# Summing y by fp32 transposes in the layout of the output projection, a buffer of its own for VectorE's product with C, and one-pair buffers for dt

## The chip, the cores and the metric

One core of one Trainium2 chip runs the whole program. The metric is the device time of one execution in microseconds (us). TensorE, VectorE, ScalarE, GpSimd and SyncE (which issues all the DMAs) run side by side and meet in semaphores. In the profile they stand as PE (matmuls) and PEld (its weight loads), DVE, ACT, POOL and SP.

## The reference, cut to what matters

All is fp32. The input is 16 sequences of 512 positions and 256 features.

```python
xr = x @ in_proj_w.T;  xf, res = split(xr, 512)
u0 = silu(conv(xf) + b);  u1 = silu(conv_b(u0) + b_b)          # two directions, d = 0 and 1
for d:   delta, B, C = split(u_d @ x_proj_w[d].T, [16, 32])
         dt = softplus(delta @ dt_proj_w[d].T + dt_proj_b[d])  # 512 channels
         dA_cum = exp(reversed cumulative sum of dt * A)       # 16 states a channel
         xs = cumsum(dt * u_d * B * dA_cum) / (dA_cum + 1e-12)
         y_d = sum over the 16 states of xs * C + u_d * D[d]
y = (y_0 + y_1) * silu(res)
x = layernorm(x + y @ out_proj_w.T)
# then a soft mixture of experts (1024 slots of 16 experts, softmax over rows and over columns)
x = layernorm(x + moe(x))
```

## The kernel before, in words

There are three stages: sequence_stage (16 sequences, a hardware loop of one turn each), expert_stage and merge_stage. The change is in the first only.

**The scan.** A sequence is worked through in 128 tiles, two tiles to a step, so 64 steps. A tile is one state of one chunk of 128 channels, 128 channels on the partitions by 512 positions. The 64 steps are four parts of 16 states: channels 0 to 255 in direction 0, then in direction 1 (tiles 0 to 63), then channels 256 to 511 in both (tiles 64 to 127). One step i goes through all engines:

- GpSimd: g = dtu * B (`inputs`, L637), into a ring of three, two steps ahead.
- ScalarE: e = exp(dt * A) into PSUM (`decay`, L802) and a guard factor f by a tanh (`guard`, L812), a step ahead.
- VectorE: the scan over positions, in place in PSUM (`scan`, L1008), then z = (f + 1) * e into z_ring, a ring of three (`guarded`, L1025).
- GpSimd: v = z * C into v_ring, a ring of three (`times_c`, L646). On every eighth step (i % 8 == 4, `ON_DVE`) VectorE does this product itself (L1034), and writes it over the step's place in z_ring.
- TensorE: adds v to y in two PSUM banks by a matmul with the identity as weights (`add_state`, L1175), six tiles later (`Y_LAG`).

Before `guarded(i)` writes its place in z_ring, it waits in `z_slot_free` (L1010) for the step that had the place last. Was that a GpSimd step, it waits for GpSimd's product; was it a VectorE step, as it is for i % 8 == 7, it waits until TensorE has added the product (`v_used`). GpSimd's product in turn waits until TensorE has added the product that stood in its place of v_ring.

**The gate.** At tiles 70 and 6 (of the next turn) VectorE multiplies a pair of y banks with `res_gate` into `yg` (`y_gate`, L991), channels on the partitions.

**The side work.** Everything else of the sequence is a list of 70 slots, written out by hand in `timetable()`: projections, convolutions, dt, the output projection, and the mixture's logits, softmaxes and slot sums. The slots take two PSUM banks in turn. `slot_tiles` gives each slot a tile, from the weights in HOLD. At that tile TensorE fills the slot's bank (`fill`, L1077, after it has waited for the bank's last reader); two to five tiles later ScalarE and VectorE read it (`side_step`, L695 and L899). All engines are in program order, so a fill that waits holds back the `add_state` calls behind it. Slots in `AHEAD` work for the next sequence. A pair of dt slots has a chain behind it, a softplus built of Abs, Exp, an addition and Ln on ScalarE, and on VectorE L926 (twice), L932, L937 and two scans for the reversed sums (`rsum`, L948), then GpSimd's dtu (L622).

**SyncE** loads a row of B and of C for each step, and four steps late it issues the side work's stores. At step 10 (`X_STEP`) it loads the next sequence's transposed x, once the res slots have read the old one.

Of the kernel before, what the change touches and what calls it, by code (L numbers as in the profile page):

```python
# [23 lines left out]
P = 128  # L24
# [96 lines left out]
def timetable():  # L121

    order = """
        dt1_0 dt1_1 out0 out1 res2 res3 dt0_2 dt0_3 xnT0 xnT1
        rows0 rows1 in0_0 in0_1 cols0 cols1 conv0_0 conv0_1 rowsT0 rowsT1 dt1_2 dt1_3 colsT0 colsT1 rows2 rows3
        conv1_0 conv1_1 slots0 slots1 cols2 cols3 rowsT2 rowsT3 colsT2 colsT3 rows4 rows5 slots2 slots3 cols4 cols5
        in0_2 in0_3 rowsT4 rowsT5 conv0_2 conv0_3 colsT4 colsT5 x0_0 rows6 conv1_2 conv1_3 rows7 dt0_0 dt0_1  # L130
        slots4 slots5 x1_0 cols6 cols7 rowsT6 rowsT7 res0 res1 colsT6 colsT7 slots6 slots7"""
    return [(name[:-1].rstrip("_"), int(name[-1])) for name in order.split()]
# [4 lines left out]
        "xnT": 2, "rows": 3, "cols": 4, "rowsT": 2, "colsT": 2, "slots": 3}  # L137
FIRST, IN_TILE, LAST_IN_TILE = 2, 28, 76
OUT_TILE, STATS_TILE, VAR_TILE, ROUGH_TILE, RSTD_TILE, APPLY_TILE = 8, 15, 18, 20, 22, 25


def slot_tiles(table, last):

    tiles, first, second = [], table.index(("rows", 0)), table.index(("in0", 2))
    for slots, begin, end in ((table[:first], FIRST, IN_TILE), (table[first:second], IN_TILE, LAST_IN_TILE),
                              (table[second:], LAST_IN_TILE, last)):
        total, before = sum(HOLD[kind] for kind, _ in slots), 0.0
        for kind, i in slots:
            tile = begin + int(before / total * (end - begin))
            if (kind, i) == ("out", 0):  # L150
                tile = max(tile, OUT_TILE)
            if (kind, i) == ("xnT", 0):
                tile = max(tile, APPLY_TILE + 2)

            tiles.append(max([tile] + tiles[-1:] + [t + 2 for t in tiles[-2:-1]]))
            before += HOLD[kind]
    return tiles
# [3 lines left out]
    ("x0", 0), ("x1", 0), ("res", 0), ("res", 1), ("dt0", 0), ("dt0", 1))  # L161
EPILOGUE = ("out", "xnT", "rows", "cols", "rowsT", "colsT", "slots")


def sequence_stage(nc, xT, x, in_wT, conv_w, conv_b, x_wT, dt_wT, A_log, D, out_wT,
# [38 lines left out]
    tile_of = slot_tiles(TABLE, TILES - 4)  # L204
# [9 lines left out]
    SP_LAG, X_STEP = 4, 10  # L214
# [48 lines left out]
    with ExitStack() as ctx:  # L263
# [30 lines left out]
        res_gate = sb("res_gate", [P, KI, L])  # L294
        xdbl = [sb(f"xdbl{d}", [XR, L]) for d in range(NDIR)]
        dt = [sb(f"dt{d}", [P, KI, L]) for d in range(NDIR)]
        dtu = [sb(f"dtu{d}", [P, KI, L]) for d in range(NDIR)]
        rsum = [sb(f"rsum{d}", [P, KI, L]) for d in range(NDIR)]
        sp_exp, sp_one = dtu, rsum
        yg = sb("yg", [P, KI, L])  # L300
# [9 lines left out]
        se = dt[0][:].rearrange("p a (b c) -> p (a b) c", c=DM)  # L310
# [7 lines left out]
        g_ring = sb("g_ring", [P, 3, 2, L])  # L318
        f_ring = sb("f_ring", [P, FR, 2, L])
# [291 lines left out]
        def _(pool):  # L611
# [4 lines left out]
            def dtu_of_chunk(at, s, i):  # L616
# [446 lines left out]
        def _(pe):  # L1063
# [13 lines left out]
            def fill(at, s):  # L1077
# [18 lines left out]
                if kind in ("in0", "res"):  # L1096
                    if kind == "in0" and i == 0:
                        pe.wait_ge(xT_loaded, at.seq(s) * 16 + 16)
# [402 lines left out]
```

## Time and profile before

| | |
|---|---|
| median of 3 runs | 6382.84 us (6379.36 to 6392.4) |
| the profiled execution's own time | 6391.75 us |
| its span | 6389.9 us |
| busy: PE, PEld | 5305.4 us (83%), 2615.8 us (41%) |
| busy: DVE, ACT, POOL | 4887.0 us (76%), 4299.3 us (67%), 4857.2 us (76%) |
| mean granted TensorE clock | 0.901 |

Busy times are shares of the whole span. GpSimd works in the sequence stage only, which ends at about 5400 us, so there its share is higher. A busy TensorE isn't a TensorE at its peak: the ends of matmuls are modelled and they overlap.

### The profile page before, as it was taken

The page shows a single profiled execution, that of the slowest core. Times are in us where ns is not written, and L with a number is a line of the kernel's source. Part 1 is how long each engine was busy: PE and PEld are TensorE (multiplying, and loading weights), DVE is VectorE, ACT ScalarE, POOL GpSimd, SP SyncE. Part 2 cuts the span into 40 slices and gives each one's busy share as a digit, 9 for nine tenths or more (in the row PEclk, how much of TensorE's full clock was granted, in tenths as well). Part 3 has the DMA queues.
Part 4 walks back from the last instruction along what each step waited for, and adds up shares of the span by engine and source line. Part 5 has one row for each costly group of instructions (what it writes and reads, how often), then busy time and mean ns, then how long its engine had stood idle before and what let it go on. Part 6 is the DMA issues. An engine that isn't in the chain of part 4 may idle for free. (4 is left out here: it accounts for less than half of the span.)

```text
span 6389.9 us, 71120 instructions
## 1 busy us (share of the span) xinstructions
PE 5305.4 (83%) x14640; PEld 2615.8 (41%) x14640; DVE 4887.0 (76%) x4310; ACT 4299.3 (67%) x6698; POOL 4857.2 (76%) x2327
## 2 busy tenths in 40 slices
PE   6878788888878787888888878787878787999977
PEld 2333333333333333334343434343434344555566
DVE  6988888888888888888888888888888882222233
ACT  4878787878778777878787878787878784111100
POOL 3999999999999999999999999999999991000000
PEclk9999998988989888889898989898989898999988
DMA  2434333333333333434343433333333332322266
GB/s 78 123 118 122 120 120 114 120 120 118 120 115 121 115 122 115 122 111 124 114 122 111 124 117 121 115 117 117 121 118 120 121 123 82 95 84 86 75 217 210
DMA packets 555713, 755.58 MB, mean 118 GB/s; under 512 B 124059, under 2 KB 272411, under 8 KB 553245
## 3 DMA queue, kind: packets, MB, share of 16 engines
q1 hardware_dynamic: 555293, 752.04, 38.0%
q14 instruction: 408, 3.34, 0.2%
q8 instruction: 12, 0.20, 0.0%
HBM read 662.04 MB, written 89.82 MB: 118 GB/s over the span
## 5 line engine op out<-in xcount | busy, mean ns | idle before, releaser
L637 POOL TENSOR_TENSOR g_ring<-dtu,b_ring 128x1024 f32<-128x1024 f32 x1026 | 2523.2, 2462 | 148.2 <-DVE e_ps L1008 107.2
L1008 DVE TENSOR_TENSOR_SCAN e_ps<-e_ps,g_ring 128x1024 f32<-128x1024 f32 x1024 | 2342.9, 2288 | 109.0 <-ACT e_ps L802 72.7
L646 POOL TENSOR_TENSOR v_ring<-z_ring,c_ring 128x1024 f32<-128x1024 f32 x896 | 2191.0, 2446 | 144.8 <-PE y_ps L1175 109.4
L1175 PE MATMUL y_ps<-v_ring,ident 128*128 128x512 f32 x3596 | 2036.0, 677 | 305.1 <-POOL v_ring L646 293.4
L802 ACT ACTIVATE e_ps<-dt,a_neg 128x512 f32<-128x512 f32 x2050 | 1398.6, 682 | 808.1 <-DVE z_ring L1025 635.2
L812 ACT ACTIVATE f_ring<-rsum,consts,a_neg_half 128x512 f32<-128x512 f32 x2050 | 1645.6, 803 | 0.8
L1025 DVE SCALAR_TENSOR_TENSOR z_ring<-f_ring,e_ps 128x1024 f32<-128x1024 f32 x896 | 1089.6, 1216 | 388.6 <-PE y_ps L1175 267.9
L1175 PEld LDWEIGHTS y_ps<-v_ring,ident 128*128 128x128 f32 x3596 | 704.8, 213 | 1186.2 <-issue 754.2
L1110 PE MATMUL side<-u,conv_diag 128*128 128x512 f32 x1088 | 503.7, 607 | 31.6 <-ACT rowT_ring L733 31.6
L1285 ACT ACTIVATE x_act<-x_gate,x_bg 128x512 f32<-128x512 f32 x128 | 87.9, 687 | 562.2 <-PE x_gate L1317 562.2
L1140 PE MATMUL side<-seT,xnT 128*128 128x512 f32 x544 | 308.9, 704 | 122.9 <-ACT xnT L727 102.4
L1160 PE MATMUL side<-dispT_ring,xn 128*128 128x128 f32 x2176 | 300.6, 297 | 121.1 <-DVE dt L926 61.3
L1299 DVE SCALAR_TENSOR_TENSOR x_hT<-x_up,x_bu,x_act 128x512 f32<-128x512 f32 x128 | 96.1, 751 | 375.8 <-PE x_up L1321 375.8
L1160 PEld LDWEIGHTS side<-dispT_ring,xn 128*128 128x128 f32 x2176 | 287.4, 210 | 203.6 <-DVE u L918 83.8
L1110 PEld LDWEIGHTS side<-u,conv_diag 128*128 128x128 f32 x1088 | 209.3, 193 | 306.6 <-issue 261.7
L1429 PE MATMUL m_acc<-m_eo,m_pT 128*128 128x256 f32 x1024 | 243.9, 404 | 65.1 <-DMA m_rinv<-rinv_scr 65.1
L1145 PE MATMUL side<-xnT,seT 128*128 128x512 f32 x544 | 257.1, 596 | 23.6 <-ACT u L705 19.7
L1101 PE MATMUL side<-xT_t,w_in 128*128 128x512 f32 x536 | 266.2, 621 | 11.4 <-DVE a_neg L896 5.3
L622 POOL TENSOR_TENSOR dtu<-dt,u 128x512 f32<-128x512 f32 x130 | 158.6, 1220 | 135.8 <-DVE rsum L948 135.3
L1317 PE MATMUL x_gate<-x_xT,x_wg 128*128 128x512 f32 x512 | 242.5, 596 | 16.0 <-DMA x_bu<-in_bu 16.0
L948 DVE TENSOR_TENSOR_SCAN rsum<-consts,dt 128x511 f32<-128x511 f32 x130 | 249.8, 1922 | 0.0
L1429 PEld LDWEIGHTS m_acc<-m_eo,m_pT 128*128 128x128 f32 x1024 | 208.6, 205 | 100.3 <-issue 68.3
(137 smaller groups left out, 5688.5 us busy)
## 6 DMA issues: line engine op xcount, KB each, us to landing
b_ring<-bc_scr SPq DMA_DIRECT2D x1027, 256.0 KB, 3.4
c_ring<-bc_scr SPq DMA_DIRECT2D x1025, 256.0 KB, 3.3
pT_scr<-rowT_ring SPq DMA_DIRECT2D x136, 256.0 KB, 3.5
m_pT<-pT_scr SPq DMA_DIRECT2D x16, 2048.0 KB, 8.4
sT_scr<-sT_ring SPq DMA_DIRECT2D x272, 64.0 KB, 2.5
x_xT<-sT_scr SPq DMA_DIRECT2D x16, 1024.0 KB, 8.8
eo_scr<-x_eo SPq DMA_DIRECT2D x32, 512.0 KB, 5.1
m_eo<-eo_scr SPq DMA_DIRECT2D x16, 1024.0 KB, 11.0
```

The source lines that it names most:

```text
L637: pool.tensor_tensor(g_ring[:, k], dtu[d][:, pair:pair + 2], both(b_ring[:, k:k + 1]), ALU.mult).then_inc(g_done, 1)
L646: pool.tensor_tensor(v_ring[:, k], z_ring[:, k], both(c_ring[:, k:k + 1]), ALU.mult).then_inc(v_pool, 1)
L802: act.activation(e_ps[:, i % 2, h], dt[d][:, c], ACT.Exp, scale=a_neg[:, d, c, n:n + 1]).then_inc(e_done, 1)
L812: act.activation(f_ring[:, i % FR, h], rsum[d][:, c], ACT.Tanh, scale=a_neg_half[:, d, c, n:n + 1], bias=guard_bias).then_inc(f_done, 1)
L1008: dve.tensor_tensor_scan(e, e, g, 0.0, ALU.mult, ALU.add).then_inc(scan_done, 1)
L1025: dve.scalar_tensor_tensor(out=z, in0=f_ring[:, i % FR], scalar=1.0, in1=e_ps[:, i % 2], op0=ALU.add, op1=ALU.mult).then_inc(z_done, 1)
L1101: mm = pe.matmul(bank, w_in[:, k, m * P:(m + 1) * P], xT_t[:, k], start=(k == 0), stop=(k == KM - 1))
L1110: mm = pe.matmul(bank, conv_diag[:, d, i, k], src[:, i, k:k + L], start=(k == 0), stop=(k == KC - 1))
L1140: mm = pe.matmul(bank, xnT[:, k, t * P:(t + 1) * P], seT[:, k, h * HS:(h + 1) * HS], start=(k == 0), stop=(k == KM - 1))
L1160: mm = pe.matmul(bank[:, k * P:(k + 1) * P], xn[:, t, k * P:(k + 1) * P], dispT_ring[:, i % 2, t * P:(t + 1) * P], start=(t == 0), stop=(t ...
L1175: pe.matmul(y_ps[:, t % 2], ident[:], v, start=(t % (TILES // PAIRS) < 2), stop=True, skip_group_check=True).then_inc(v_used, 1)
L1429: mm = pe.matmul(acc[:, q, t, 0:DM], pT[q][:, s, t * P:(t + 1) * P], eo[q][:, s], start=(s == 0), stop=(s == ST - 1))
```

## The change

Four things are changed, all in sequence_stage.

- **y by transposes.** `add_state` no longer multiplies the identity with v. It makes four transposes of 128x128 blocks (v as weights, the identity moving, `is_transpose=True`) that add in PSUM, so that y stands with positions on the partitions. The skip terms (`SKIPS`, L1187) are four matmuls of 128 columns each instead of one of 512. `res` is computed in that layout too (xT as weights), and the gate writes in place over `res_gate` (`yg = res_gate`). The output projection needs the channels on the partitions, so four new slots `yT` transpose the gated y back, each with four transposes, and ScalarE copies each out of PSUM.
- **VectorE's product with C** goes into `v_own`, a buffer of its own; before it is written, VectorE waits for TensorE's add of its last product, eight steps earlier. A place in z_ring now waits for GpSimd's product alone.
- **One-pair buffers.** dt, dtu and rsum hold one pair of chunks a direction instead of two, so a pair is computed only after the part that used the last one. The dt slots stand at tiles 1 and 4, 36 and 36, 66 and 68, 97 and 100 (before: 2 and 5, 18 and 21, 43 and 45, 97 and 100).
- **The table.** All four res slots are now of the current sequence, behind the output projection. 74 slots instead of 70; tiles are spread between anchors (`EARLIEST`). The first layer norm starts at tile 20 instead of 15 and is applied at 30 instead of 25; the logits start at tile 34 instead of 29. X_STEP is 18.

```diff
-        dt1_0 dt1_1 out0 out1 res2 res3 dt0_2 dt0_3 xnT0 xnT1
-        rows0 rows1 in0_0 in0_1 cols0 cols1 conv0_0 conv0_1 rowsT0 rowsT1 dt1_2 dt1_3 colsT0 colsT1 rows2 rows3
...
-        slots4 slots5 x1_0 cols6 cols7 rowsT6 rowsT7 res0 res1 colsT6 colsT7 slots6 slots7"""
+        dt1_0 dt1_1 yT0 yT1 out0 yT2 yT3 out1 res0 res1 res2 res3 xnT0 xnT1
+        rows0 rows1 dt0_2 dt0_3 in0_0 in0_1 cols0 cols1 conv0_0 conv0_1 rowsT0 rowsT1 colsT0 colsT1 rows2 rows3
+        conv1_0 conv1_1 slots0 slots1 cols2 cols3 rowsT2 rowsT3 colsT2 colsT3 rows4 rows5 dt1_2 dt1_3 slots2 slots3
...
+STATS_TILE, VAR_TILE, ROUGH_TILE, RSTD_TILE, APPLY_TILE = 20, 23, 25, 27, 30
+EARLIEST = {("dt1", 0): 1, ("yT", 0): 8, ("xnT", 0): APPLY_TILE + 2, ("dt0", 2): 34, ("dt1", 2): 66, ("in0", 2): 79,
+            ("dt0", 0): 97, ("slots", 7): 122}
+def slot_tiles(table):
+    anchors = [s for s, slot in enumerate(table) if slot in EARLIEST]
+    tiles = []
+    for s, slot in enumerate(table):
+        first = max(a for a in anchors if a <= s)
+        after = min([a for a in anchors if a > s], default=first)
+        tile = EARLIEST[table[first]]
+        if after > first:
+            hold = [HOLD[kind] for kind, _ in table[first:after]]
+            tile += int((EARLIEST[table[after]] - tile) * sum(hold[:s - first]) / sum(hold))
+        tiles.append(max([tile] + tiles[-1:] + [t + 2 for t in tiles[-2:-1]]))
...
-    SP_LAG, X_STEP = 4, 10
+    SP_LAG, X_STEP = 4, 18
+    def dve_step_before(i):
+        return max(j for j in range(i - STEPS, i) if on_dve(j))
...
-        dt = [sb(f"dt{d}", [P, KI, L]) for d in range(NDIR)]
+        dt = [sb(f"dt{d}", [P, 2, L]) for d in range(NDIR)]
-        yg = sb("yg", [P, KI, L])
+        yg = res_gate
+        ygT = sb("ygT", [P, 2, KI, P])
+        v_own = sb("v_own", [P, 2, L])
...
+                    elif kind == "yT":
+                        act.activation(ygT[:, i % 2], src.rearrange("p (c l) -> p c l", c=KI), ACT.Copy).then_inc(free, 1)
...
                 def z_slot_free(i):
-                    user = before(i)
-                    if on_dve(user):
-                        dve.wait_ge(v_used, b * TILES + (2 * (user + 1) + CR))
-                    else:
-                        dve.wait_ge(v_pool, b * (STEPS - len(ON_DVE)) + (pool_steps(user + 1) + CR))
+                    dve.wait_ge(v_pool, b * (STEPS - len(ON_DVE)) + (pool_steps(last_on_pool(before(i)) + 1) + CR))
...
-                    z_slot_free(i)
-                    dve.tensor_tensor(z_ring[:, k], e_ps[:, i % 2], both(c_ring[:, k:k + 1]), ALU.mult).then_inc(v_dve, 1)
+                    dve.wait_ge(v_used, b * TILES + (2 * (dve_step_before(i) + 1) + CR))
+                    dve.tensor_tensor(v_own[:], e_ps[:, i % 2], both(c_ring[:, k:k + 1]), ALU.mult).then_inc(v_dve, 1)
...
+                elif kind == "yT":
+                    if i == 0:
+                        pe.wait_ge(y_gated, at.seq(s) * 2 + 1)
+                    for c in range(KI):
+                        mm = pe.transpose(bank[:, c * P:(c + 1) * P], yg[:, i, c * P:(c + 1) * P], ident[:])
...
-                pe.matmul(y_ps[:, t % 2], ident[:], v, start=(t % (TILES // PAIRS) < 2),
-                          stop=True, skip_group_check=True).then_inc(v_used, 1)
+                for lb in range(LT):
+                    mm = pe.matmul(rows_of(lb, t % 2), v[:, lb * P:(lb + 1) * P], ident[:], is_transpose=True,
+                                   start=(t % (TILES // PAIRS) == 0 and lb % 2 == 0), stop=True, skip_group_check=True)
+                mm.then_inc(v_used, 1)
```

## Rows read from the trace of the kernel before

**Rows 1.** The page's head: span, then busy us (share) xinstructions of each engine.
```profile
span 6389.9 us, 71120 instructions
PE 5305.4 (83%) x14640; PEld 2615.8 (41%) x14640; DVE 4887.0 (76%) x4310; ACT 4299.3 (67%) x6698; POOL 4857.2 (76%) x2327
```

**Rows 2.** Busy time by stretch, columns in the first row: fourteen sequences.
```profile
core 0: us, PE busy (x) PEld busy (x) DVE busy (x) ACT busy (x) POOL busy (x), PEclk, DMA share, GB/s
735.00:5295.00 4560.00, 3756.12 (x9746) 1710.41 (x9745) 3991.81 (x2997) 3612.70 (x5629) 4242.69 (x2017) 0.89 0.39 119
```

**Rows 3.** Waits of POOL, 735 to 5295 us: waiter <- releaser: us in total, times, longest.
```profile
POOL v_ring L646 <- PE y_ps L1175: 103.3, 74, 3.0
POOL g_ring L637 <- DVE e_ps L1008: 95.1, 77, 4.5
POOL dtu L622 <- DVE rsum L948: 36.8, 28, 2.2
POOL g_ring L637 <- DMA b_ring<-bc_scr: 34.9, 11, 4.2
POOL v_ring L646 <- DVE z_ring L1025: 29.5, 22, 2.5
```

**Rows 4.** Waits of DVE, the same stretch.
```profile
DVE z_ring L1025 <- PE y_ps L1175: 242.1, 70, 8.3
DVE e_ps L1008 <- ACT e_ps L802: 65.5, 31, 5.6
DVE yg L991 <- PE y_ps L1175: 38.3, 14, 3.5
```

**Rows 5.** Groups by form, same stretch: count | busy us, mean ns | idle before, releasers.
```profile
L637 POOL TENSOR_TENSOR g_ring<-dtu,b_ring 128x1024 f32<-128x1024 f32 x897 | 2209.1, 2466 | 132.4 <-DVE e_ps L1008 95.1 <-DMA b_ring<-bc_scr 34.9 <-issue 1.0
L1008 DVE TENSOR_TENSOR_SCAN e_ps<-e_ps,g_ring 128x1024 f32<-128x1024 f32 x896 | 2050.1, 2288 | 95.6 <-ACT e_ps L802 65.5 <-POOL g_ring L637 30.1
L646 POOL TENSOR_TENSOR v_ring<-z_ring,c_ring 128x1024 f32<-128x1024 f32 x784 | 1916.4, 2445 | 133.4 <-PE y_ps L1175 103.3 <-DVE z_ring L1025 29.5
L948 DVE TENSOR_TENSOR_SCAN rsum<-consts,dt 128x511 f32<-128x511 f32 x112 | 217.5, 1942 | 0.0
L932 DVE SCALAR_TENSOR_TENSOR dtu<-rsum,dt 128x1024 f32<-128x1024 f32 x56 | 114.6, 2046 | 35.3 <-ACT rsum L750 35.3
L733 ACT ACTIVATE rowT_ring<-side 128x512 f32<-128x512 f32 x112 | 64.6, 577 | 0.0
```

**Rows 6.** Timeline of PE at 1028 us, clock 1.00: start, us, instruction, [idle before].
```profile
1028.42 0.65 PE L1150 MATMUL side<-ident,row_t 128*128 128x128 f32 x4 [2.81 <-ACT disp_ring L763]
1028.91 1.02 PE L1175 MATMUL y_ps<-v_ring,ident 128*128 128x512 f32 x2
```

**Rows 7.** Timeline of PE at 1307 us.
```profile
1307.81 3.60 PE L1110 MATMUL side<-u,conv_diag 128*128 128x512 f32 x8
1311.24 1.88 PE L1175 MATMUL y_ps<-z_ring,ident 128*128 128x512 f32 x4
1312.96 1.02 PE L1175 MATMUL y_ps<-v_ring,ident 128*128 128x512 f32 x2
```

**Rows 8.** Timeline of DVE, the same moment.
```profile
1305.57 2.29 DVE L1008 TENSOR_TENSOR_SCAN e_ps<-e_ps,g_ring 128x1024 f32<-128x1024 f32 x1
1313.16 1.22 DVE L1025 SCALAR_TENSOR_TENSOR z_ring<-f_ring,e_ps 128x1024 f32<-128x1024 f32 x1 [5.30 <-PE y_ps L1175]
```

**Rows 9.** Timeline of PE at 2547 us, clock 0.50.
```profile
2546.92 1.11 PE L1150 MATMUL side<-ident,row_t 128*128 128x128 f32 x4 [2.75 <-ACT disp_ring L763]
2547.83 1.91 PE L1175 MATMUL y_ps<-v_ring,ident 128*128 128x512 f32 x2
```

**Rows 10.** Busy time by stretch, columns as in Rows 2: one sequence's tiles 0-7, 80-95.
```profile
1063.70:1081.00 17.30, 13.04 (x16) 4.45 (x16) 15.61 (x11) 11.17 (x18) 13.21 (x7) 0.60 0.45 132
1277.70:1314.90 37.20, 34.30 (x89) 14.82 (x87) 30.44 (x22) 29.55 (x46) 36.06 (x17) 1.00 0.41 138
```

**Rows 11.** DMA issues: KB each, median us to landing.
```profile
xT_t<-in_x_T SPq DMA_DIRECT2D x17, 512.0 KB, 4.7
```

More of the change, by code:

```diff
@@ L136 @@
 HOLD = {"out": 3, "res": 4, "conv0": 4.5, "conv1": 4.5, "x0": 3, "x1": 3, "dt0": 5, "dt1": 5, "in0": 3,
[L137 to L156, printed above, removed]
+        "xnT": 2, "yT": 2.5, "rows": 3, "cols": 4, "rowsT": 2, "colsT": 2, "slots": 3}
@@ L157, in slot_tiles @@
     return tiles
 AHEAD = tuple((kind, i) for kind in ("in0", "conv0", "conv1") for i in range(4)) + (
-    ("x0", 0), ("x1", 0), ("res", 0), ("res", 1), ("dt0", 0), ("dt0", 1))
-EPILOGUE = ("out", "xnT", "rows", "cols", "rowsT", "colsT", "slots")
+    ("x0", 0), ("x1", 0), ("dt0", 0), ("dt0", 1))
+EPILOGUE = ("yT", "out", "xnT", "rows", "cols", "rowsT", "colsT", "slots")
 def sequence_stage(nc, xT, x, in_wT, conv_w, conv_b, x_wT, dt_wT, A_log, D, out_wT,
@@ L293, in sequence_stage @@
         xf_pad = u[1]
-        res_gate = sb("res_gate", [P, KI, L])
+        res_gate = sb("res_gate", [P, LT, DI])
         xdbl = [sb(f"xdbl{d}", [XR, L]) for d in range(NDIR)]
-        dt = [sb(f"dt{d}", [P, KI, L]) for d in range(NDIR)]
-        dtu = [sb(f"dtu{d}", [P, KI, L]) for d in range(NDIR)]
-        rsum = [sb(f"rsum{d}", [P, KI, L]) for d in range(NDIR)]
+        dt = [sb(f"dt{d}", [P, 2, L]) for d in range(NDIR)]
+        dtu = [sb(f"dtu{d}", [P, 2, L]) for d in range(NDIR)]
+        rsum = [sb(f"rsum{d}", [P, 2, L]) for d in range(NDIR)]
         sp_exp, sp_one = dtu, rsum
-        yg = sb("yg", [P, KI, L])
+        yg = res_gate
+        ygT = sb("ygT", [P, 2, KI, P])
         x1 = sb("x1", [P, LT, DM])
@@ L636, in inputs @@
                 pool.wait_ge(scan_done, b * STEPS + (before(gi) + 1 + CR))
-                pool.tensor_tensor(g_ring[:, k], dtu[d][:, pair:pair + 2], both(b_ring[:, k:k + 1]),
+                pool.tensor_tensor(g_ring[:, k], dtu[d][:], both(b_ring[:, k:k + 1]),
                                    ALU.mult).then_inc(g_done, 1)
@@ L1095, in fill @@
                 pe.wait_ge(side_free[at.bank(s)], at.freed(s, 0))
-                if kind in ("in0", "res"):
-                    if kind == "in0" and i == 0:
+                if kind == "in0":
+                    if i == 0:
                         pe.wait_ge(xT_loaded, at.seq(s) * 16 + 16)
-                    m = i if kind == "in0" else KI + i
                     for k in range(KM):
-                        mm = pe.matmul(bank, w_in[:, k, m * P:(m + 1) * P], xT_t[:, k], start=(k == 0), stop=(k == KM - 1))
+                        mm = pe.matmul(bank, w_in[:, k, i * P:(i + 1) * P], xT_t[:, k], start=(k == 0), stop=(k == KM - 1))
+                elif kind == "res":
+                    for k in range(KM):
+                        mm = pe.matmul(bank, xT_t[:, k, i * P:(i + 1) * P], w_in[:, k, DI:2 * DI],
+                                       start=(k == 0), stop=(k == KM - 1))
+                elif kind == "yT":
+                    if i == 0:
+                        pe.wait_ge(y_gated, at.seq(s) * 2 + 1)
+                    for c in range(KI):
+                        mm = pe.transpose(bank[:, c * P:(c + 1) * P], yg[:, i, c * P:(c + 1) * P], ident[:])
                 elif kind in ("conv0", "conv1"):
@@ L1185, in _ @@
                     for d, q, pair in SKIPS.get(turn, ()):
-                        pe.matmul(y_ps[:, q], d_diag[:, d, 2 * pair + q], u[d][:, 2 * pair + q, PAD:],
-                                  start=False, stop=True, skip_group_check=True)
+                        for lb in range(LT):
+                            pe.matmul(rows_of(lb, q), u[d][:, 2 * pair + q, PAD + lb * P:PAD + (lb + 1) * P],
+                                      d_diag[:, d, 2 * pair + q], start=False, stop=True, skip_group_check=True)
                     for s in range(SLOTS):
```

60 lines of the change are left out of this document (31 added, 29 removed).

## The prediction

> **What bounds the kernel now.** I read the page's head first, then the busy time of a stretch of whole sequences, then who waits for whom on the two fullest engines, and last the timeline at the longest wait.
>
> The head makes TensorE the fullest engine, 83% of the span [rows 1]. That is misleading: the other stages are in it, and busy TensorE time stretches with the clock. The stretch from 735 to 5295 us holds 896 scans [rows 5], 64 a sequence, so 14 sequences of 4560 / 14 = 325.7 us each. In it GpSimd is busy 4242.7 us, 303.0 a sequence or 93%; VectorE 285.1, TensorE 268.3, ScalarE 258.1 [rows 2]. GpSimd's two products take 2.47 + 2.45 = 4.91 us a step, VectorE's scan and guard 2.29 + 1.22 = 3.51 [rows 5, 8], with the side work on top. So GpSimd is the bound, with VectorE close behind, and what a sequence can lose is GpSimd's idle time: 325.7 - 303.0 = 22.7 us.
>
> That idle time has owners [rows 3]. Per sequence (divide by 14): 7.4 us waiting for TensorE's add, 8.9 for VectorE (6.8 for the scan that frees g's place, 2.1 for z), 2.6 for rsum, 2.5 for the load of B. That names 21.4 of the 22.7.
>
> VectorE is late partly because it waits itself: 242.1 / 14 = 17.3 us a sequence at z for TensorE, in 70 / 14 = 5 waits, and 2.7 at the gate [rows 4]. These are the steps whose place in z_ring was last a VectorE step's. The timeline shows the largest kind: the scan ends at 1307.86, z starts at 1313.16, after TensorE has gone through a convolution (3.43 us from start to start) and the adds [rows 7, 8].
>
> **TensorE's price, part by part.** A full fp32 add shows as two records; four records take 1312.96 - 1311.24 = 1.72 us, so 0.86 a tile [rows 7]. Four transposes of 128x128 take 1028.91 - 1028.42 = 0.49 us until the next instruction [rows 6]. At half clock the four take 0.91 [rows 9]. The trace of before has no transposes that add into PSUM; I take the price of those that overwrite, as they have the same operands. Bounds: at best one of the two records of now, 0.43; at worst what the real matmul costs, 0.86, for no gain. 0.49 is the value of the nearest row.
>
> - Adds: 128 x (0.86 - 0.49) = 47.4 us less a sequence on TensorE.
> - yT: 4 x 0.49 = 2.0 us more. The skip terms keep their columns, 8 x 512; res and the output projection too. I count these as zero, plus up to 1 us for extra weight loads.
> - ScalarE: four more copies of 0.58 [rows 5], 2.3 us; it is busy 258 of 326, so GpSimd's products hide them. Uncovered they would cost 2.3.
> - VectorE: the same instructions; product and gate only change addresses.
> - TensorE's need at full clock was about 268.3 x 0.89 = 239 us [rows 2], and becomes 239 - 47 + 3 = 195.
>
> **VectorE's waits.** With v_own, z waits for a GpSimd product at least three steps back. The wait that comes instead, for TensorE's add of eight steps earlier, is over long before. So 17.3 us of stalls go from VectorE. They don't go from the span: GpSimd is 18 us fuller a sequence than VectorE [rows 2], so most of them turn into VectorE waiting for g. What counts is GpSimd's 8.9 us for VectorE. The rings let the two drift apart by two steps, 2 x 4.91 = 9.8 us. A dt pair puts about 2 x 1.94 + 2 x 2.05 = 8.0 us [rows 5] and its two PSUM reads on VectorE within some ten tiles. In those five steps VectorE's lead, 1.4 us a step, gives back 7, and the drift covers what is left; stalls like the 5.3 us on top are what empties it. Without them I take 2.0 for the 8.9. Ends: 0 and 8.9.
>
> **GpSimd's wait for TensorE**, 7.4. Fewer TensorE microseconds alone would take it to about 2: between two adds of a place of v_ring stand six tiles, 6 x 0.37 = 2.2 us less, and the mean wait is 103.3 / 74 = 1.4 [rows 3]. Two things speak against the whole. First the clock: it is granted by how full TensorE is. At tiles 0 to 7, where TensorE is busy 13.0 of 17.3 us, it is 0.60; at tiles 80 to 95, with 34.3 of 37.2, it is 1.00 [rows 10]. With a fifth less work more stretches fall to 0.50, and there the transposes (0.91) cost no less than the full matmul does now, and a convolution twice its 3.43. Second the table: at tile 36 stand both dt slots of a pair and at 38 both in slots, whose banks VectorE frees in its step of tile 40. The in fills wait for it and hold the adds of turns 39 to 41; GpSimd's v of step 19 waits for turn 39. That is a scan, two reads of 0.7 us and 3.4 us of matmuls, some 7 us after z, but it falls into a dt burst, in which GpSimd would wait for VectorE anyway. I take 5.5 for the 7.4. Ends: 1 and 15.
>
> The Trainium skill says in TensorE: Matmul & The Clock Gate, Part 4, that transpose mode "doesn't count as PE-busy the same way" for the full clock. No row here shows a long run of transposes. By that rule the adds would no longer hold the clock up; the time that this would give is worked out below as the slower rival, from rows alone.
>
> **What stays.** 2.6 for rsum: dtu still follows the two scans. 2.5 for the load of B, always at the head of a turn, behind SyncE's store of the last slots; slots_7 stays at tile 122. The load of the next x moves from step 10 to 18 on SyncE's queue, behind eight more loads of B and C; it lands in 4.7 us [rows 11], and its user, in0_0 at tile 38, waits for tile 40 anyway. Free, and at worst 3 us. The layer norm starts five tiles later with the same distances; ScalarE's stop there (VectorE <- ScalarE, 65.5 / 14 = 4.7 [rows 4]) stays. The prologue loses two res slots beside GpSimd's first products: nothing. After the last turn the output projection waits for transposes and copies twice: 2 x (2 x 0.49 + 0.58 + 0.3 for semaphores, my estimate), about 4 us.
>
> **The sum.** Idle of GpSimd a sequence: 5.5 + 2.0 + 2.6 + 2.5 + 1.3 unnamed = 13.9 instead of 22.7. Saved: 8.8 x 16 = 141 us; less 4 at the end. The profiled execution took 6391.75 us, so 6391.75 - 137 = 6255. It stood 8.9 above the median of the runs, so 6246 for a run.
>
> **The rivals.**
> - *All waits for TensorE go.* If the clock holds, GpSimd's wait for it falls to 1 and that for VectorE to 0: idle 7.4, 15.3 x 16 = 245 saved, 6383 - 245 + 4 = 6142. For it: GpSimd's waits are short (mean 1.4). Against: the clock's rows.
> - *The stalls change their owner.* The clock drops and fills wait in the tighter table (the first half of the logits stands in tiles 34 to 63, and had 29 to 66): GpSimd's waits for TensorE grow to 9 to 11 and those for VectorE fall to 5 only. Idle 20.4 to 22.4, 5 to 37 us saved and 4 lost: 6350 to 6385. For it: rows 10. Against: VectorE's own five waits are gone whatever TensorE does.
> - *TensorE becomes the bound: slower.* Its need is 195 us at full clock. Below a mean granted clock of 195 / 317 = 0.61 in the loop it needs more than GpSimd allows. At 0.56 it is 348 a sequence, 348 - 325.7 = 22 x 16 = 357 more: 6740; at 0.58, 336: 6550. For it: 0.60 is granted now where TensorE is busy three quarters of the time. Against: when TensorE is the bound it is never idle, and the only clock seen beside a full TensorE is 1.00; the convolutions and logits remain, real matmuls.
> - *No change by transposes*: if they cost 0.86, TensorE stays at 239 + 3 under a denser table; VectorE's waits still go. Idle 9 + 3 + 6.4 = 18.4, 69 saved, 6318.
>
> **How the numbers follow.** The forecast has 0.50 (6190 to 6310), all waits gone 0.18, changed owner 0.16, transposes at full price 0.05, slower 0.11. A measurement of this kernel tells 0.2%, 13 us, from no change. Faster takes the first two whole, the transposes' case and about two thirds of the changed owner: 0.84; same 0.05; slower 0.11. The range reaches from just above the best rival to the end of the changed owner: 6150 to 6385, and leaves out the slower case and half of the best one.
>
> **What would show it.** In the new trace: the add in four records of transposes a tile, TensorE's busy time down by 30 us or more a sequence; no wait of z for y_ps; VectorE's idle time now ahead of scans, released by g; GpSimd at 96% in the loop; its waits for y_ps at one place near step 19; a granted clock of 0.75 to 0.85 in the loop. Wrong it would be if the clock fell under 0.65 with TensorE over 95% busy, or if GpSimd's waits for TensorE grew above 10 us a sequence.

## The result: slower by 0.28%, and the profile after

The changed kernel took 6409.5 us (median of 9 runs, 6401.5 to 6411.7), the kernel before 6391.6 on the same chip: a ratio of 1.0028, 95% interval 1.0018 to 1.0038. The forecast was 6246 us, with 0.84 on faster. The time lies outside the range, on the side that had 0.11, and not by the mechanism given there. The profiled execution took 6410.96 us, 19 us more than that of before.

The page's head of the changed kernel, to be held against [rows 1]:

```profile
span 6409.1 us, 81593 instructions
PE 4703.2 (73%) x19780; PEld 3133.2 (49%) x19780; DVE 5080.2 (79%) x4307; ACT 4325.9 (67%) x6764; POOL 4819.2 (75%) x2327
```

The same stretch of the loop, columns as in [rows 2]:

```profile
735.00:5295.00 4560.00, 3211.57 (x14239) 2155.88 (x14240) 4169.64 (x2998) 3635.25 (x5689) 4211.70 (x2019) 0.80 0.39 119
```

TensorE's busy time falls from 3756 to 3212 us, 39 a sequence, and the granted clock from 0.89 to 0.80. VectorE's busy time rises by 178 us, 12.7 a sequence, though it has the same instructions (2998 in the stretch, 2997 before). GpSimd, the bound, is busy 300.8 us a sequence and idle 24.9; before it was 303.0 and 22.7. So a sequence takes as long as it did. Who owns GpSimd's idle time now (us in total, times, longest; divide by 14), against [rows 3]:

```profile
POOL g_ring L641 <- DVE e_ps L1012: 123.9, 28, 4.5
POOL v_ring L650 <- PE y_ps L1190: 95.9, 35, 5.1
POOL dtu L626 <- DVE rsum L951: 66.9, 41, 1.8
POOL g_ring L641 <- DMA b_ring<-bc_scr: 29.4, 18, 3.3
POOL g_ring L641 <- issue: 17.6, 12, 2.0
```

The first row is to be read by its count: before, 77 waits of 1.2 us on average; now 28, two a sequence, of 4.4. They stand at g of step 40 in all 14 turns and at g of step 56 in 13 of them. And VectorE's own idle time has fallen from 40.6 to 27.9 us a sequence, and its waits for TensorE's adds, 242.1 us before, are gone (33.3 us for TensorE are left, ahead of L913, the residual sum behind the output projection). Its largest waits, against [rows 4]:

```profile
DVE e_ps L1012 <- ACT e_ps L807: 100.5, 111, 2.9
DVE z_ring L1025 <- DVE e_ps L1012: 89.9, 469, 0.2
```

An engine without a stall that makes the bound wait: its busy time must hold one. The groups by form of VectorE in the same stretch (count | busy us, mean ns | idle before) show where, against L932 in [rows 5]:

```profile
L935 DVE SCALAR_TENSOR_TENSOR dtu<-rsum,dt 128x1024 f32<-128x1024 f32 x56 | 289.8, 5175 | 0.0
L951 DVE TENSOR_TENSOR_SCAN rsum<-consts,dt 128x511 f32<-128x511 f32 x112 | 191.8, 1713 | 0.0
L940 DVE TENSOR_TENSOR dt<-rsum,dtu 128x1024 f32<-128x1024 f32 x56 | 128.2, 2290 | 18.8 <-ACT rsum L760 18.8
```

L935, which I call the fix (the first of the two VectorE operations that finish a pair of softplus chunks; L932 before), has the same shape and took 2.05 us on average before; now it takes 5.18. Its four places in a turn are very unequal: median 1.8 us in step 4, 2.9 in step 20, 9.0 in step 36 and 7.6 in step 52. The timeline of VectorE at a fix of step 36 (start, duration):

```profile
1908.89 1.22 DVE L1025 SCALAR_TENSOR_TENSOR e_ps<-f_ring,e_ps 128x1024 f32<-128x1024 f32 x1
1910.02 9.05 DVE L935 SCALAR_TENSOR_TENSOR dtu<-rsum,dt 128x1024 f32<-128x1024 f32 x1
1918.99 1.21 DVE L1034 TENSOR_TENSOR v_own<-e_ps,c_ring 128x1024 f32<-128x1024 f32 x1
1920.12 2.28 DVE L1012 TENSOR_TENSOR_SCAN e_ps<-e_ps,g_ring 128x1024 f32<-128x1024 f32 x1
```

and of GpSimd at the same moment:

```profile
1908.69 2.36 POOL L650 TENSOR_TENSOR v_ring<-z_ring,c_ring 128x1024 f32<-128x1024 f32 x1
1911.01 2.35 POOL L641 TENSOR_TENSOR g_ring<-dtu,b_ring 128x1024 f32<-128x1024 f32 x1
1913.33 2.34 POOL L650 TENSOR_TENSOR v_ring<-z_ring,c_ring 128x1024 f32<-128x1024 f32 x1
1915.64 2.34 POOL L641 TENSOR_TENSOR g_ring<-dtu,b_ring 128x1024 f32<-128x1024 f32 x1
1922.49 2.35 POOL L641 TENSOR_TENSOR g_ring<-dtu,b_ring 128x1024 f32<-128x1024 f32 x1 [4.51 <-DVE e_ps L1012]
```

Four products follow each other without a gap. The last ends at 1917.98, the fix 1.09 us later, about what it takes by itself. It got through only when GpSimd had run out of input, in all 14 turns of step 36 and in 13 of step 52; by then VectorE's lead is spent, and GpSimd stands 4.51 us for the scan behind it. Where the fix passes, it waits for the product that is running and goes next, and the price is the other way round (VectorE, then GpSimd, in step 4):

```profile
1748.16 1.28 DVE L935 SCALAR_TENSOR_TENSOR dtu<-rsum,dt 128x1024 f32<-128x1024 f32 x1
```

```profile
1745.99 2.36 POOL L641 TENSOR_TENSOR g_ring<-dtu,b_ring 128x1024 f32<-128x1024 f32 x1
1748.32 3.32 POOL L650 TENSOR_TENSOR v_ring<-z_ring,c_ring 128x1024 f32<-128x1024 f32 x1
```

There the product pays, with 3.32 us instead of 2.35, and GpSimd has no gap here either. That is the common case. The subtraction L940, which also has two operands in SBUF, went so in all 56 cases of the stretch (at 1.8 to 2.9 us), here in step 37, VectorE and then GpSimd:

```profile
1924.13 1.79 DVE L940 TENSOR_TENSOR dt<-rsum,dtu 128x1024 f32<-128x1024 f32 x1 [0.31 <-ACT rsum L760]
1924.79 3.34 POOL L650 TENSOR_TENSOR v_ring<-z_ring,c_ring 128x1024 f32<-128x1024 f32 x1
```

In the kernel before, 46 of the 56 fixes went so, and 8 met an idle GpSimd. In its step 13 there is no gap of GpSimd ahead of the fix or behind it (the second row of GpSimd is two products, of 2.35 and 3.3 us):

```profile
1463.16 2.57 DVE L932 SCALAR_TENSOR_TENSOR dtu<-rsum,dt 128x1024 f32<-128x1024 f32 x1 [2.68 <-ACT rsum L750]
1459.98 2.35 POOL L646 TENSOR_TENSOR v_ring<-z_ring,c_ring 128x1024 f32<-128x1024 f32 x1
1462.29 5.66 POOL L637 TENSOR_TENSOR g_ring<-dtu,b_ring 128x1024 f32<-128x1024 f32 x2
1467.91 2.34 POOL L646 TENSOR_TENSOR v_ring<-z_ring,c_ring 128x1024 f32<-128x1024 f32 x1
```

So products that follow each other without a gap can keep the fix out, but don't always.

**Where the 19 us come from.** Read off the timeline of scans: the first scan is 2.8 us later, the sixteen turns are 10.9 us longer, 8.7 more lie between the last scan and the experts, and the expert and merge stages take 3.1 less. Measured from first scan to first scan, turns 2 to 15 take 325.5 us on average against 325.9, 5.9 us less together, which the first turn gives back (324.6 against 318.7). What is left is the last turn, from its first scan to its last: 309.2 us before, 320.0 now. Those 10.8 us decide between slower and no change. They lie with the kernel before: over the same 63 steps its turns 2 to 15 take 318.75 us on average and the changed kernel's 318.1. So it is mostly the last turn of before that is short, by 9.5 us, as its first two are (311.7 and 311.5), and less the new one that is long, by 1.9. Why those are short is open.

### The profile page after: what moved, and what is told of

Read it like the earlier page. It is cut to its first block and busy times, and to the rows that moved or that the text cites. A ratio compares the mean times of both kernels' runs of the same rounds, so it can differ in the third digit from the quotient of the medians.

```text
span 6409.1 us, 81593 instructions
## 1 busy us (share of the span) xinstructions
PE 4703.2 (73%) x19780; PEld 3133.2 (49%) x19780; DVE 5080.2 (79%) x4307; ACT 4325.9 (67%) x6764; POOL 4819.2 (75%) x2327
## 5 line engine op out<-in xcount | busy, mean ns | idle before, releaser
L641 POOL TENSOR_TENSOR g_ring<-dtu,b_ring 128x1024 f32<-128x1024 f32 x1026 | 2478.7, 2420 | 194.1 <-DVE e_ps L1012 145.2
L1190 PE MATMUL y_ps<-ident,v_ring 128*128 128x128 f32 x7192 | 1214.1, 310 | 594.4 <-POOL v_ring L650 552.6
L1190 PEld LDWEIGHTS y_ps<-ident,v_ring 128*128 128x128 f32 x7192 | 979.2, 161 | 1058.5 <-POOL v_ring L650 577.6
L1159 PE MATMUL side<-xnT,seT 128*128 128x512 f32 x544 | 313.7, 708 | 272.1 <-ACT sT_ring L746 272.1
L1174 PE MATMUL side<-dispT_ring,xn 128*128 128x128 f32 x2176 | 352.9, 331 | 63.1 <-DVE dt L929 63.1
L1174 PEld LDWEIGHTS side<-dispT_ring,xn 128*128 128x128 f32 x2176 | 335.0, 243 | 78.6 <-DVE dt L929 76.9
L935 DVE SCALAR_TENSOR_TENSOR dtu<-rsum,dt 128x1024 f32<-128x1024 f32 x65 | 329.5, 5069 | 0.5 <-ACT rsum L755 0.5
L1140 PE MATMUL side<-w_out,ygT 128*128 128x256 f32 x544 | 191.1, 527 | 159.8 <-ACT ygT L730 159.8
L1159 PEld LDWEIGHTS side<-xnT,seT 128*128 128x128 f32 x544 | 108.9, 222 | 365.5 <-ACT sT_ring L746 280.3
L1104 PE MATMUL side<-xT_t,w_in 128*128 128x512 f32 x272 | 181.7, 817 | 139.6 <-DVE dt L929 84.5
## 6 DMA issues: line engine op xcount, KB each, us to landing
m_eo<-eo_scr SPq DMA_DIRECT2D x16, 1024.0 KB, 10.9
```

The source lines that it names most:

```text
L641: pool.tensor_tensor(g_ring[:, k], dtu[d][:], both(b_ring[:, k:k + 1]), ALU.mult).then_inc(g_done, 1)
L935: dve.scalar_tensor_tensor(out=sp_exp[d][:], in0=sp_one[d][:], scalar=1.0, in1=dt[d][:], op0=ALU.subtract, op1=ALU.subtract).then_inc(fix_ ...
L1159: mm = pe.matmul(bank, seT[:, k, i * P:(i + 1) * P], xnT[:, k], start=(k == 0), stop=(k == KM - 1))
L1174: mm = pe.matmul(bank[:, k * P:(k + 1) * P], xn[:, t, k * P:(k + 1) * P], dispT_ring[:, i % 2, t * P:(t + 1) * P], start=(t == 0), stop=(t ...
L1190: mm = pe.matmul(rows_of(lb, t % 2), v[:, lb * P:(lb + 1) * P], ident[:], is_transpose=True, start=(t % (TILES // PAIRS) == 0 and lb % 2 = ...
```

## The experiments

Medians in us, ratios to the kernel before on the same chip with their 95% intervals (those without were run once). A "turn" is the mean from first scan to first scan, turns 2 to 15; the clock is the mean granted clock of TensorE in that part of the loop.

| run | us | ratio | turn | clock, loop |
|---|---|---|---|---|
| own_alone | 6311.9 | 0.987 (0.986-0.989) | 320.5 | 0.89 |
| yield_fix | 6292.5 | 0.984 (0.983-0.986) | 318.2 | 0.81 |
| real_adds | 6331.2 | 0.990 (0.989-0.992) | 322.0 | 0.93 |
| real_yield | 6308.2 | 0.989 (0.987-0.990) | 319.3 | 0.94 |
| real_yield_in0 | 6368.8 | 0.997 (0.996-0.998) | 323.5 | 0.93 |
| yield_in0 | 6335.1 | 0.993 (0.991-0.994) | 321.8 | 0.82 |
| own_yield | 6193.5 | 0.970 (0.968-0.972) | 313.0 | 0.91 |
| own_yield_transposes | 6196.4 | 0.968 (0.966-0.970) | 313.1 | 0.81 |
| own_yield_early_end | 6214.5 | 0.971 (0.969-0.973) | 314.0 | 0.91 |
| before_yield | 6431.8 | 1.007 (1.005-1.008) | 327.7 | 0.89 |
| fix_one_column | 6385.5 | once | 323.8 | 0.80 |
| fix_one_input | 6410.9 | once | 325.6 | 0.80 |
| fix_reduce | 6328.6 | once | 320.6 | 0.81 |

**own_alone**: one part of the change, on the kernel before. yg stays one buffer over res_gate, where the next res overwrites the first pair's gated y; that part of the computation differs.

```diff
-dve.tensor_tensor(z_ring[:, k], e_ps[:, i % 2], ...C, ALU.mult)
+dve.wait_ge(v_used, ...dve_step_before(i)...)
+dve.tensor_tensor(v_own[:], e_ps[:, i % 2], ...C, ALU.mult)
```

> The kernel before with one part of the change alone: VectorE's product with C in its own buffer (and the gated y written over res_gate, to make room). Theory H (a two-input SBUF operation of VectorE gets no turn while GpSimd's products follow each other without a gap): VectorE's five waits at z for y_ps, 17.3 us a sequence, go; VectorE runs ahead, GpSimd stands behind it with work queued, and L932's mean grows from 2.05 us to 3.5 or more; the total falls by 20 to 80 us only. Rival D (the prediction's: drift between the engines covers the dt bursts): L932 stays at 2.0 to 2.4 and the total falls by about 100 to 140 us.

1.3% faster, about 80 us, at the very end of what the first theory allowed. No wait of z for TensorE is left. The fix's group (same form as L932 in [rows 5]):

```profile
L936 DVE SCALAR_TENSOR_TENSOR dtu<-rsum,dt 128x1024 f32<-128x1024 f32 x52 | 261.8, 5034 | 35.0 <-ACT rsum L755 35.0
```

So the long fixes, 7.7 and 8.6 us at steps 25 and 52, come with v_own alone, without the new table or the transposes: VectorE is rid of its five stalls, and at two places of a turn GpSimd now keeps it out. At steps 5 and 13 the fix stays at 1.3 and 2.6 us (medians), so VectorE's lead alone doesn't say where it is kept out.

**yield_fix**: the changed kernel, with GpSimd made to wait for the fix once before g of step 38, and once behind g of step 54. 

```diff
+for kind in YIELD_BEFORE.get(i, ()):     # {36: dt1 of chunk 3}
+    pool.wait_ge(fix_done, at.pair(TABLE.index(kind)))
 inputs(b, i + G_AHEAD)
+for kind in YIELD_AFTER.get(i, ()):      # {52: dt0 of chunk 1}
+    pool.wait_ge(fix_done, at.pair(TABLE.index(kind)))
```

> The changed kernel, in which GpSimd waits for L935's result at two places of each sequence: before g of step 38 and after g of step 54, where L935 now takes 9.0 and 7.6 us (medians). Theory H: with GpSimd stopped L935 takes 1.2 to 3.5 us there, GpSimd loses about 1.5 us at each of the two waits but the stops of 4.5 us before g of step 40 and 4.2 us before g of step 56 all but go: net 3 to 6 us a sequence, 50 to 100 us in all, against the changed kernel's 6410. Rival M (L935 is slow by itself, from the new buffers' places or its operands): it stays at 8 to 9 us and the total grows by 16 x 2 x 6 = 190 us.

GpSimd's waits, 735 to 4900 us (13.1 turns):

```profile
POOL v_ring L652 <- PE y_ps L1196: 80.9, 27, 5.4
POOL dtu L628 <- DVE rsum L957: 39.2, 26, 1.8
POOL v_ring L652 <- DVE dtu L941: 16.1, 13, 1.2
POOL g_ring L643 <- DVE dtu L941: 16.1, 13, 1.2
POOL g_ring L643 <- DVE e_ps L1018: 7.4, 4, 2.6
```

The fix takes 2.0 us at step 36 and 5.6 at step 52, where GpSimd's wait stands behind one more product. Two waits of 1.2 us take the place of two of 4.4: those for the scans go from 8.9 to 0.6 us a sequence, and the change is 1.6% faster than before instead of 0.3% slower. This is the step that failed, mended by itself: 7.3 us a turn and some 117 us in all.

**fix_one_column**: is it the fix's own work?

```diff
-out=sp_exp[d][:], in0=sp_one[d][:], ... in1=dt[d][:]
+out=sp_exp[d][:, 1 - d, (L - 1) * d:(L - 1) * d + 1], in0=sp_one[d][...the same...], in1=dt[d][...the same...]
```

> The changed kernel with L935 on one column of 1024 (and L940 adding instead of subtracting, to keep dt positive; the correction of the softplus is so left out). Theory H: the operation still reads two operands from SBUF, so at steps 36 and 52 it still takes 6 to 9 us although its own work is under 0.1 us. Rival M (its size or its buffers cost the time): under 1 us everywhere.

No. One column, and it still takes 7.6 us at step 36 and 6.5 at step 52; where it passes, 0.15 (735 to 4900 us):

```profile
L935 DVE SCALAR_TENSOR_TENSOR dtu<-rsum,dt 128x1 f32<-128x1 f32 x51 | 185.8, 3643 | 0.0
```

**fix_one_input** and **fix_reduce**: which property keeps it out. In both, as in fix_one_column, the subtraction two tiles behind becomes an addition, and a small correction of the softplus is left out.

```diff
-dve.scalar_tensor_tensor(out=sp_exp[d][:], in0=sp_one[d][:], scalar=1.0, in1=dt[d][:], ...)
+dve.tensor_scalar(sp_exp[d][:], sp_one[d][:], -1.0, None, ALU.add)           # fix_one_input
+dve.tensor_reduce(sp_exp[d][:, 0, 0:1], sp_one[d][:], XY, ALU.max)           # fix_reduce
```

> The changed kernel with the softplus's fix on VectorE given one SBUF operand instead of two (it computes sp_one - 1 and the step after it adds; the small correction of softplus is left out, so dt is slightly off). Theory, that a VectorE operation with two SBUF operands gets no turn while GpSimd's products follow each other: the fix takes 1.3 us or less everywhere, and the blocked time moves to the next operation with two SBUF operands, the subtraction behind it, which then has mean 3.5 to 5 us with some of 7 to 9; g of steps 40 and 56 still wait some 4 us each, a turn stays at 323 to 326 us, the time 6370 to 6415. Rival, that it is something about that one operation (its scalar form, its place behind ScalarE): both take under 2.2 us, g's two waits go, a turn of 317 to 319 and a time of 6280 to 6300.

> The changed kernel with the softplus's fix on VectorE replaced by a maximum over the same 128x1024 of sp_one (one SBUF operand, one column written), and the subtraction behind it by an addition; softplus's small correction is left out, so dt is off. The run fix_one_input did not separate the theories: its tensor_scalar took 0.69 us where nothing was beside it, twice as fast as one element a cycle, so it took a second port as well, and it still took 8.5 and 7.1 us at steps 36 and 52. A reduction has no such faster form. Theory (what is kept waiting is an operation that needs VectorE's second read port, which it shares with GpSimd): the reduction takes 1.1 to 1.4 us at all four places, and the next operation with two SBUF operands, the addition two tiles later, is kept waiting in its place, 6 to 9 us at steps 37 and 53; the scans' wait and g's waits at steps 40 and 56 stay near 4 us each, a turn 323 to 327 us, 6370 to 6415. Rival (it is the place behind ScalarE or the time at which VectorE has run ahead, whatever it issues): the reduction itself takes 6 to 9 us at steps 36 and 52.

The first missed: with one SBUF operand the fix still took 8.5 and 7.1 us, so "two operands" is not the whole property. Unhindered it takes 0.69 us where the two-operand form takes 1.2, so this form runs at about twice the rate, and such a form is kept out as well. fix_reduce has neither property. Its groups, 735 to 4900 us:

```profile
L939 DVE TENSOR_TENSOR dt<-rsum,dtu 128x1024 f32<-128x1024 f32 x52 | 245.3, 4717 | 17.6 <-ACT rsum L760 17.6
L935 DVE TENSOR_REDUCE dtu<-rsum 128x1 f32<-128x1024 f32 x52 | 63.0, 1212 | 0.0
```

At the same place and moment the reduction takes 1.21 us every time, and the two-operand addition two tiles behind it takes the blocked time over (7.0 and 6.7 us at steps 37 and 53), as the theory had it; the rival of place and moment falls. The size was off: 320.6 us a turn and 6329 us, not 323 to 327 and 6370 to 6415. g's waits for the scans at steps 40 and 56 are gone; the dtu waits for rsum grow instead (to 145.1 us in the stretch, from 4.8 to 11.2 a turn). The Trainium skill says in SBUF — State Buffer, Who interferes with whom, that VectorE contends with a GpSimd instruction that reads SBUF when it has two SBUF inputs or runs in a mode that uses two ports, that a reduction never does, and that the loser "fully blocks". All three runs agree with that. The wait measured here goes further: not through one product but through up to four, 9 us for 1.1 us of work.

**real_adds**: the changed kernel with the adds as real matmuls in the new layout, to give the clock back.

```diff
-mm = pe.matmul(rows_of(lb, t % 2), v[:, lb * P:(lb + 1) * P], ident[:], is_transpose=True,
+mm = pe.matmul(rows_of(lb, t % 2), v[:, lb * P:(lb + 1) * P], ident[:],
```

> The changed kernel with is_transpose left out, so that each tile is added by four real fp32 matmuls of 128 columns, with the same result. By the rows of before a 128-column matmul costs 0.24 us, so 0.97 a tile instead of 0.49: TensorE busy up by about 60 us a sequence, granted clock in the loop back from 0.80 to 0.90 or more. If TensorE's time is what GpSimd waits for, the total grows by 100 us or more; if (theory H) the loop is bound by GpSimd and by VectorE's blocked operations, it grows by less than 60 us.

1.2% faster than the changed kernel, where I had expected a loss of up to 60 us; and TensorE's busy time rises by 33 us a turn, not 60. It looks like the clock (0.93 in the loop, with TensorE busy 262.4 us a turn against 229.2). The waits say something else as well: v's at step 19 falls from 4.0 to 1.25 us, but the fix of step 36 takes 3.2 us instead of 9.0. So two effects are mixed, and three more runs were to separate them.

**real_yield**, **real_yield_in0** and **yield_in0**: real adds with both waits (before g of steps 38 and 54), and the anchor ("in0", 0): 40 on top, with real adds and with transposes (the latter on yield_fix's kernel, its second wait put before g of step 54).

> The changed kernel with both: real matmuls for the adds, and GpSimd waiting for L935 before g of step 38 and before g of step 54. Theory H+C (the blocked operations and the lower clock each cost what was measured alone, 117 and 78 us against the changed kernel): the two add up nearly, 6410 - 117 - 60 = about 6230, the granted clock in the loop at 0.92 or more, no stop of GpSimd at g of steps 40 and 56. Rival (the real adds help only because TensorE's slower adds keep VectorE from running ahead, so that the yields take their place): no better than 6290.

> The same, and the in0 slots anchored at tile 40 instead of 38, the tile at which VectorE frees their banks. If the wait of v of step 19 for y_ps (1.3 us with real adds, 4.0 with transposes) comes from the in0 fills that wait two tiles ahead, it goes, and the total is 10 to 25 us below real_yield. Rival: the wait only moves to the next tight slots, rowsT at tile 48, and the total is the same within 10 us.

> The changed kernel with its transposes, the two waits of GpSimd and in0 at tile 40. Against yield_fix (6293): the 3.8 us of v19 should fall to 1 to 2, 30 to 45 us in all, if the place in the table makes that wait; if the low clock makes it (a fill takes twice as long wherever it stands), under 15 us.

Once GpSimd yields, real adds buy nothing: 6308 against 6293 us with transposes, nearer the rival than the 6230 of the theory. But the two aren't alike in all else: with real adds the wait ahead of g of step 38 costs 6.2 us (1.2 in yield_fix), which I read as VectorE being late there, and the second wait stands before g of step 54, not behind it. Moving in0 to tile 40, where the prediction saw its fill held up, makes both worse, by 61 and 43 us, which no expectation had: it puts the fix in step 21, where it takes 7.9 and 6.2 us, and v's waits for TensorE move to steps 22 to 29 and grow. A table that is moved to cure one wait moves the fix too.

**own_yield**: the kernel before, v_own, yg in a buffer of its own for the first pair and in place for the second, and both waits (before g of steps 27 and 54). Old table, old dt buffers, real adds.

```diff
+YIELD_BEFORE = {25: (('dt1', 3),), 52: (('dt0', 1),)}
-dve.tensor_tensor(yg[:, pair], y_ps[:], res_gate[:, pair], ALU.mult)
+dve.tensor_tensor(yg[:] if p == 0 else res_gate[:, pair], y_ps[:], res_gate[:, pair], ALU.mult)
```

> The kernel before with two things: VectorE's product in its own buffer (nothing left out this time), and GpSimd waiting for the fix of the dt pair before g of step 27 and before g of step 54. No transposes, no one-pair buffers, the old table. Theory H: own_alone's two blocked operations (7.7 and 8.6 us) fall to 2 to 3.5, its stops of 4.5 and 2.3 us go, and the total is 6312 - 16 x 5 = about 6235. If this is as fast as real_yield, then the transposes' layout, the one-pair buffers and the new table have brought nothing by themselves; theory C says so. If the new table is worth something, own_yield is 20 us or more slower than real_yield.

It beats both kernels: 6193.5 us, 3.0% under before, and some 40 us better than the theory had it. GpSimd's waits, 735 to 4900 us:

```profile
POOL g_ring L644 <- DMA b_ring<-bc_scr: 47.2, 13, 4.4
POOL g_ring L644 <- DVE dtu L943: 43.3, 26, 2.3
POOL dtu L629 <- DVE rsum L959: 16.2, 14, 1.2
POOL g_ring L644 <- DVE e_ps L1019: 5.5, 9, 1.0
POOL v_ring L653 <- PE y_ps L1182: 2.9, 8, 0.9
```

TensorE's part has fallen from 7.4 to 0.2 us a sequence with the same adds at the same price; own_alone already had it at 1.4. So those waits, too, hung on VectorE's stalls.

**own_yield_transposes** and **before_yield**, the two counterparts: own_yield with the adds as transposes (gate and output projection left as they are, so y's values differ), and the kernel before with the two waits alone.

```diff
-pe.matmul(y_ps[:, t % 2], ident[:], v, ...)
+for lb in range(LT):
+    mm = pe.matmul(y_ps[:, t % 2, lb * P:(lb + 1) * P], v[:, lb * P:(lb + 1) * P], ident[:], is_transpose=True, ...)
```

> The version own_yield (the kernel before with v_own and the two waits, 6193.5 us) with one thing more: each add of y is four transposes of 128x128 (v's block as the stationary operand, the identity moving) into the same columns of y_ps, so y's blocks come out transposed in this run and its values differ; the table, the dt buffers and the output projection stay as before. This takes the transposed adds alone, without the denser table. My theory: with GpSimd no longer held by VectorE, the transposes take TensorE's busy time down by 30 to 35 us a sequence (261 to about 228) and the granted clock in the loop from 0.91 to 0.80, and the two about cancel: GpSimd's idle time for TensorE at v rises from 0.2 to 1 to 3 us a sequence, a turn is 314 to 316 us instead of 313.0, the time 6205 to 6240. The rival, that fewer busy microseconds on TensorE are a gain or nothing: v's waits stay at 0.2, a turn of 312 to 313, 6175 to 6195. A second rival, that the lower clock is what costs the changed kernel most of its 5.2 us a turn against own_yield: a turn of 318, 6270 or more.

> The kernel before with nothing but the two waits that own_yield has (GpSimd waits for the fix before g of steps 27 and 54), without v_own. If the waits are worth something only where VectorE runs ahead (its fixes take 1.2 to 2.6 us in the kernel before, of which little can go), the time stays within 0.5% of before: 6365 to 6405 us. Rival, that the waits by themselves are worth the 118 us that own_yield is under own_alone: 6270 to 6300.

The transposes take 448 us of busy time from TensorE, 34 a turn, and the clock from 0.91 to 0.81, own_yield first:

```profile
735.00:4900.00 4165.00, 3469.20 (x9214) 1588.41 (x9215) 3838.73 (x2855) 3417.80 (x5339) 4035.07 (x1927) 0.91 0.40 123
```

```profile
735.00:4900.00 4165.00, 3021.12 (x12619) 1935.25 (x12620) 3832.96 (x2854) 3420.82 (x5338) 4038.93 (x1926) 0.81 0.41 124
```

and change the time not at all (turns of 313.1 and 313.0; the intervals overlap). My theory of a cost of 1 to 3 us a turn missed, as did the second rival; the first came true but for one microsecond. GpSimd never waits for TensorE in this run, so neither less work on TensorE nor the lower clock is worth anything here. The Trainium skill's TensorE: Matmul & The Clock Gate, Part 4, has it that transpose mode doesn't count as busy time for the full clock in the way that matmuls do; both pairs of runs with and without transposes agree (0.93 to 0.80, 0.91 to 0.81). But TensorE's busy time falls in both as well, and no run tells the two apart; and here no time hangs on it.

before_yield is 0.65% slower, outside what I gave: GpSimd stands 138.2 us in 25 waits for the fix, 5.2 us at g of step 27 and 5.9 at g of step 54. z's waits for TensorE are still there (217.4 us), and I read it so that VectorE, stalled by them, is late where GpSimd waits. So the waits cost without v_own, and v_own gives less than half of what the two give together without them.

**own_yield_early_end**: the last slots of a turn three tiles earlier (`slot_tiles(TABLE, TILES - 7)`), for the wait for B.

> own_yield with the last slots of a turn three tiles earlier (the layer norm's and slots' order of tiles ends at tile 121 less 2 instead of 124 less 2), so that SyncE's store at the end of a turn comes earlier and with it the load of B for g of step 3, which is GpSimd's largest idle time left (3.8 us a sequence). The slot of the second dt of the first pair moves from tile 100 to 99. My theory: that wait shrinks by 2 to 3.5 us a turn, nothing else changes: 6140 to 6165 us. Rival: the load is bound by the store's own length or by the queue, and the wait stays at 3.8 or moves to the layer norm's start: 6185 to 6200.

Missed: g of step 3 still waits 3.6 us for B (3.8 in own_yield), 0.7 us of waits for TensorE come back at step 45, and a turn is 1.0 us longer. What bounds that load is open.

## Why the prediction was wrong, by its own steps

- *GpSimd is the bound, and what can be lost is its idle time*: right. So was *VectorE's five waits for TensorE go*.
- *The drift covers what is left, 2.0 for the 8.9*: this is the step that failed. Measured, 123.9 / 14 = 8.9. The burst of a dt pair was summed at 8.0 us, with the fix at its mean of 2.05 [rows 5]; at steps 36 and 52 the fix alone takes 9.0 and 7.6. The mean was that of a VectorE which stalled often, and taking the stalls away makes the fix long: own_alone, with v_own and the gated y's place as its only changes, has its mean at 5.03. That VectorE's wait can depend on its own lead had no term in the sum. yield_fix shows that the rest follows from it: with the fix let in, the term is 0.6 us. By what way the stalls had kept the fix short isn't shown. It wasn't mainly that GpSimd ran out of input: in the kernel before, 46 of 56 fixes were let in between two products without a gap.
- *2.6 stays for rsum*: 66.9 / 14 = 4.8, now in steps 22, 38 and 54 instead of 15 and 54. *2.5 for the load of B*: 2.1, plus 1.3 of issue.
- *5.5 for TensorE's adds*: 6.9, at v of step 19 (4.0, the place foreseen) and of step 22 (2.4, not foreseen).
- *The end, 4 us*: 8.7 behind the last scan; the 2.8 ahead of the first scan and the 10.8 of the last turn had no term.
- TensorE's side was right in size: busy time down 39 us a sequence (30 or more foreseen), clock 0.80 (0.75 to 0.85). But that GpSimd would be at 96% failed: it is at 92%. And that TensorE's work is a cost of the kernel at all failed: in own_yield GpSimd is nearly free of it with real adds, and with transposes it gains nothing.
- By the idle time, 11.0 us a turn are missing against the forecast's 13.9: 6.9 for scans, 2.2 for rsum, 1.4 for adds, 0.5 the rest. GpSimd's products take 2.2 us less, as fewer are lengthened by an operation of VectorE that passes (134 over 2.6 us in the stretch instead of 167), so the 8.8 us a turn that should have been saved are gone, 141 in all; with the turns' own 10.9, and the ends (2.8 + 8.7 - 4 - 3.1 = 4.4), that is the 156 us between forecast and run of the profiled executions.
- Of the rivals, *the stalls change their owner* came nearest in time (it had 20.4 to 22.4 us of idle; 24.9 measured; its time was 6350 to 6385), but by another way: the owner is VectorE, not TensorE, and not by fills.

**What the parts are worth.** v_own alone is about -80 us; with the two waits, -190; the waits alone, +34. The transposes are worth 0 on own_yield; on the changed kernel with its waits no pair differs in them alone. The rest (dt buffers of one pair, the new table, the gate in the new layout) costs: yield_fix against own_yield_transposes is 6292.5 to 6196.4, 5.1 us a turn in turns 2 to 15, 71 together, and some 25 in the first and the last turn and at the ends. v's waits at steps 19 and 22 are 6.3 us a turn there, more than the whole, so some of it is paid back elsewhere. Which of the three it is was not tried, and the two runs also have their waits at different places.

## What to carry to other kernels

Before taking a stall away from an engine, look at what its operations cost when it has run ahead. A group whose mean is well above that of another of the same shape (here 2.05 us for the fix against 1.22 for z, [rows 5, 8]) may be waiting inside its busy time, and that wait can grow when the engines' order changes. Look at it place by place, not by the mean. Where GpSimd is the bound and a trace shows it keeping out a short VectorE operation with two operands in SBUF, let GpSimd wait for that operation once, on purpose (1.2 us), rather than the other way round (9 us); but put the wait where VectorE is ahead, or it costs 5 to 6 us itself.

## What the runs showed of the hardware

- A VectorE operation with two SBUF operands, or one at double rate, waits for the GpSimd product that is running, and then mostly goes next: all 56 subtractions of the changed kernel's 14 turns, 1.8 to 2.9 us. The product behind it takes 3.3 us instead of 2.35.
- It can also be passed over: 31 of the 56 fixes waited through two to four products, 9.05 us for 1.1 us of work, and 7.6 us for one column. A reduction (1.21 us), and operations with one operand in PSUM (1.21 to 1.22), are not held up.
- What decides between the two is open. A gap between GpSimd's products is not needed to be let in (step 4 here, step 13 of the kernel before).
- In own_yield_transposes the clock granted in the loop fell from 0.91 to 0.81 and TensorE's busy time by 34 us a turn, while the kernel's time stayed the same.
